# Parting the tail norms' row operations by maxima, and loading the tail's rows and first tile behind the rotation's table

## What is computed

```python
h = _layernorm(x, axis=-1) * (1 + ca) + sa
x = x + ga * _L0_attn_ref(h, W_qkv, b_qkv, W_proj, b_proj)   # causal, 16 heads of 32, rotary q and k
h = _layernorm(x, axis=-1) * (1 + cb) + sb
x = x + gb * _L0_ffn_ref(h, ...)
```

## Time and profile before

| | |
|---|---|
| median of 3 runs | 3283.07 us (3282.28 to 3283.45) |
| profiled execution: its own time | 3289.78 us |
| its span, first to last instruction | 3288.0 us |
| mean granted TensorE clock | 0.962 |
| TensorE busy | 3013.8 us, 92% |
| VectorE busy | 2501.4 us, 76% |
| ScalarE busy | 1849.9 us, 56% |
| GpSimd busy | 1588.9 us, 48% |

### The profile page before, as it was taken

One profiled execution on the slowest core, in us unless ns is written; L12 is line 12 of the kernel. 1 busy time (PEld: TensorE's weight loads), 2 busy tenths in 40 slices (PEclk: granted clock), 3 DMA queues, 4 the chain that ended last, 5 costly groups with the idle time before them and its releaser, 6 DMA issues.

```text
span 3288.0 us, 59164 instructions
## 1 busy us (share of the span) xinstructions
PE 3013.8 (92%) x21664; PEld 1155.9 (35%) x21664; DVE 2501.4 (76%) x4214; ACT 1849.9 (56%) x3651; POOL 1588.9 (48%) x1586
## 2 busy tenths in 40 slices
PE   3799999999989999999998999999998999999896
PEld 1324343434343433434333242433324343242222
DVE  4697777777768788777877878777886878878477
ACT  3416565786655554785455555587545555455541
POOL 2303434482616465382644726365471645627355
PEclk8759999999999999999999999999999999999997
DMA  5403030413041220413113041311314122031122
GB/s 210 107 6 70 11 75 14 101 39 76 14 104 40 61 66 24 98 43 86 39 47 100 27 95 33 80 54 42 83 36 114 39 56 59 30 75 46 55 74 65
DMA packets 180875, 205.27 MB, mean 62 GB/s; under 512 B 21460, under 2 KB 137428, under 8 KB 179428
## 3 DMA queue, kind: packets, MB, share of 16 engines
q1 hardware_dynamic: 180584, 201.50, 23.4%
HBM read 114.09 MB, written 36.50 MB: 46 GB/s over the span
## 4 chain that ended last, share of the span: by engine, by line
PE 46%; issue 19%; DVE 16%; POOL 6%; POOLq 5%; DVEq 3%; ACT 3%; DMA 1%; SPq 1%; ACTq 1%
PE ring L1147 10%; PE ps_out L1197 9%; DVE mpart L902 9%; PE ps_scores L1183 7%; PE ps_scores L1121 5%; PE ps_den L1214 4%; PE ps_den L1220 3%; PE ring L1169 3%; POOL psum L529 3%; PE ps_scores L1133 2%; POOL psum L528 2%; DVE wk L948 1%; DVE dsum L918 1%; DVE wk L946 1%; POOLq L502 1%
## 5 line engine op out<-in xcount | busy, mean ns | idle before, releaser
L730 ACT ACTIVATE prob<-ps_scores 128x512 f32<-128x512 f32 (+3 forms) x2560 | 1257.8, 537 | 981.9 <-PE ps_scores L1186 477.2
L902 DVE TENSOR_REDUCE mpart<-ring 128x1 f32<-128x512 f32 (+3 forms) x2560 | 1403.1, 599 | 344.4 <-PE ring L1147 179.5
L1147 PE MATMUL ring<-qk 96*128 96x512 f16 (+3 forms) x2560 | 876.7, 365 | 73.6 <-DVE mpart L902 56.3
L1183 PE MATMUL ps_scores<-qk 98*128 98x512 f16 (+3 forms) x2560 | 867.2, 352 | 55.7 <-ACT prob L730 28.4
L528 POOL TENSOR_TENSOR psum<-prob 128x512 f32<-128x512 f32 x360 | 481.7, 1338 | 391.9 <-ACT prob L730 299.9
L1197 PE MATMUL ps_out<-prob,v 128*32 128x512 f32 (+3 forms) x5120 | 607.6, 547 | 0.0
L1147 PEld LDWEIGHTS ring<-qk 96*128 96x128 f16 x2560 | 236.1, 98 | 887.3 <-DVE mpart L902 625.2
L529 POOL TENSOR_TENSOR psum<-prob 128x512 f32<-128x512 f32 x360 | 483.4, 1343 | 0.0
L1183 PEld LDWEIGHTS ps_scores<-qk 98*128 98x128 f16 x2560 | 247.1, 99 | 370.1 <-ACT prob L730 215.7
L1121 PE MATMUL ps_scores<-hT,wg 128*128 128x512 f16 x1536 | 345.6, 382 | 3.5 <-POOL hT L519 3.5
L547 POOL TENSOR_TENSOR xs<-xs,bc 128x512 f32<-128x512 f32 x60 | 77.4, 1289 | 383.4 <-DMA xs<-in_L_attn_x_dram 382.1
(11 more groups left out here) (126 smaller groups left out, 2719.7 us busy)
## 6 DMA issues: line engine op xcount, KB each, us to landing
qk<-half SPq DMA_DIRECT2D x384, 128.0 KB, 3.6
turn<-in_rope_dram SPq DMA_DIRECT2D x64, 512.0 KB, 4.7
xs<-in_L_attn_x_dram SPq DMA_DIRECT2D x124, 256.0 KB, 2.8
attn_out_T<-ot SPq DMA_DIRECT2D x63, 256.0 KB, 2.2
otin<-attn_out_T SPq DMA_DIRECT2D x30, 512.0 KB, 4.8
out_dram<-x SPq DMA_DIRECT2D x60, 256.0 KB, 2.1
wg<-w_qkv_halves SPq DMA_DIRECT2D x16, 768.0 KB, 5.6
qk<-in_L_wmod_dram SPq DMA_DIRECT2D x1, 6144.0 KB, 26.8
```

Of the source, the lines that this page charges most:

```text
L730: act.activation(prob[:, s % 3, p, h % 2, 0:w], ps_scores[(HG * s + h) % NBK][:, 0:w], ACT.Exp, scale=SCALE).then_inc(exp_done, 1)
L902: dve.tensor_reduce(mpart[:, h, qt, kc:kc + 1], ring[use % NBK][:, 0:w], AX.X, ALU.max).then_inc(ring_free, 1)
L1147: mm = pe.matmul(ring[use % NBK][:, 0:w], qk[0:R, G % 2, 0, h, qt * P:(qt + 1) * P], qk[0:R, G % 2, 1, h, kc * QC:kc * QC + w], start=True ...
L1183: mm = pe.matmul(ps_scores[k % NBK][:, 0:w], qk[0:RM, par, 1, h, kt * P:(kt + 1) * P], qk[0:RM, par, 0, h, cq * QC + q0:(cq + 1) * QC], st ...
```

## The change

It has two parts. On SyncE, the rows of the modulation are loaded by a function of their own, in the qkv jobs of chunk 0, behind the two DMAs of the maxima rows and before chunk 0's copies; the first tile's loads (otin and x) move behind the table of chunk 3 and the q copies of chunk 2. For batch 3's own tiles the row load stays where it was. On VectorE, parts 2 and 4 of a tail tile issue their first operation only; the second one follows in the same step behind the third and fourth maximum, with the drain ahead of it. The reciprocals of parts 0 and 2 now follow the third maximum, those of parts 1 and 3 and the head's statistics the fourth.

```diff
-            def qkv(G, before, tail_load):
+            def qkv(G, before, row_load, tail_load):
                 for c in range(NC_):
                     if c > 0:
                         stack_halves(G, c - 1, 1)
-                    if c == 2:
-                        tail_load()
                     if G < NG * B - 1 or c < NC_ - 1:
                         load_turn(NC_ * G + c + 1)
                     if c == 0 and before is not None:
                         maxima_rows(before, before % 2)
+                    if c == 0:
+                        row_load()
                     stack_halves(G, c, 0)
+                    if c == 2:
+                        tail_load()
                 stack_halves(G, NC_ - 1, 1)
...
+            def rows_load(b):
+                sp.wait_ge(tail_done, wait_value(NT * b))
+                sp.wait_ge(mod_st, 32)
+                sp.dma_start(bc[:], mod_d[b, 2:8, :].rearrange("(a m) n -> a m n", a=1).to_broadcast(
+                    [P, 6, C])).then_inc(bc_ld, 16)
+
             def tail_loads(b, t, xs_use, count):
                 Z = NT * b + t
-                if t == 0:
-                    sp.wait_ge(tail_done, wait_value(Z))
-                    sp.wait_ge(mod_st, 32)
-                    sp.dma_start(bc[:], mod_d[b, 2:8, :].rearrange("(a m) n -> a m n", a=1).to_broadcast(
-                        [P, 6, C])).then_inc(bc_ld, 16)
...
+                    def row_load():
+                        if 0 in tail.values():
+                            rows_load(b - 1)
...
-                        qkv(NG * b + g + 1, NG * b + g, lambda: tail_load(FIRST_TAIL))
+                        qkv(NG * b + g + 1, NG * b + g, row_load, lambda: tail_load(FIRST_TAIL))
...
+                        if s + 2 in own and own[s + 2] == 0:
+                            rows_load(b)
...
                     dve.wait_ge(tail_rstd1, Z + 1)
                     dve.scalar_tensor_tensor(wk[:, i, :], x1[:, i, :], mv[:, i, 0:1], bc[:, 2, :], ALU.subtract, ALU.mult)
+                elif stage == 3:
                     dve.drain()
-                    dve.scalar_tensor_tensor(wk[:, i, :], wk[:, i, :], rstd[:, i, :], bc[:, 3, :], ALU.mult, ALU.add)
-                    dve.drain()
-                elif stage == 3:
                     dve.bn_stats(stats[:, i, :], wk[:, i, :])
                     dve.drain()
                     dve.bn_aggr(mv2[:, i, :], stats[:, i, :]).then_inc(tail_stats2, 1)
                 else:
-                    tail_third(b, t)
+                    dve.wait_ge(tail_rstd2, Z + 1)
+                    dve.scalar_tensor_tensor(wk[:, i, :], wk[:, i, :], mv2[:, i, 0:1], bc[:, 4, :], ALU.subtract, ALU.mult)
+
+            def tail_second_row(b, t, stage):
+                i = t % 2
+                dve.drain()
+                if stage == 2:
+                    dve.scalar_tensor_tensor(wk[:, i, :], wk[:, i, :], rstd[:, i, :], bc[:, 3, :], ALU.mult, ALU.add)
+                else:
+                    dve.wait_ge(tail_x1_shift, NT * b + t + 1)
+                    dve.scalar_tensor_tensor(x1[:, i, :], wk[:, i, :], rstd2[:, i, :], xs[:, i, :], ALU.mult,
+                                             ALU.add).then_inc(tail_done, 1)
...
-                        out_parts(G, g, s, (0, 2), first, bool(own))
                         for u, h in units[2:3]:
                             unit_max(h, u, n)
                             n += 1
+                        out_parts(G, g, s, (0, 2), first, bool(own))
+                        for u, h in units[3:4]:
+                            unit_max(h, u, n)
+                            n += 1
+                        for stage in (2, 4):
+                            if s - 2 * stage in tail:
+                                tail_second_row(b - 1, tail[s - 2 * stage], stage)
                         if s + 2 in head:
...
-                        for u, h in units[3:]:
+                        for u, h in units[4:]:
```

More of the change, by code:

```diff
@@ L467, in _ @@
             load_turn(0)
-            qkv(0, None, lambda: None)
+            qkv(0, None, lambda: None, lambda: None)
             load_group(1)
```

## The result

The changed kernel takes 3263.36 us (median of 5 runs, 3261.23 to 3268.94) beside 3282.28 us for the kernel before on the same chip: a ratio of 0.995, 95% interval 0.9939 to 0.996. It is faster, by 19 us where 40 were forecast.

A forecast was written before the change was run, and what follows sets the result against it. TensorE was taken as the bound, busy 3013.8 of 3288.0 us. Loads net 24.1 plus row pairs 20.3 gave 44.4 off 3289.8, so 3245.4; less 2.4, 3243. Own range 3226 to 3258; 8 in 10, 3224 to 3268.

The forecast's parts named there:

- the removed cost of the table: Steps 0 to 2 of nine stages: excess over a clean stage goes once the rotation table loads earlier, 38.2 us.
- step 30 of the six-tile stages: Projection's bank comes free earlier: 1.7 us in each of three stages, plus 2.5 for one fallen clock.
- step 24: Five-tile stages: third maximum ahead of the second row, with GpSimd quiet, gains 0.66 us a stage.
- Signs of "wrong": ScalarE's copy wait up over 25 us, TensorE idle in first stages' qkv jobs, stalls one matmul later, long step 0 ScalarE wait.
- the two single rivals: First, row pairs give nothing: 3263, chance 0.15. Second, copies stand behind the whole row load: 3264, chance 0.13.
- the tile loads: Standing between chunk 2's two sets of copies, they hold back the second set: 5.1 us lost over six stages.
- the third rival: Chunk 2's second copies land late behind tile loads, holding step 1's exponentials: 9.7 us each of six stages, 3297, chance 0.05.
- the row load: Ahead of chunk 0's copies it delays them 3.3 us; 3.0 us lost per first stage, 9.0 in all.
- the pairs: Third maximum before the second row: steps 16, 20, 24, 34 gain 2.26 us per five-tile stage; pairs total 20.3.
- in all other such steps there are two or fewer and nothing is parted: Outside the listed steps with a row pair, at most two maxima occur, so the new order changes nothing.
- Step 18: Six-tile stages: VectorE waits for the unfilled third maximum, holding up the second row; 0.3 us lost each, 0.9 in all.
- the profile's own: Of the 6.7 us between profiled execution and median, 2.4 us taken as profile excess and subtracted.

The follow-up runs named there:

- experiment 5: Changed kernel with the row load and the first tile's loads both at chunk 0, ahead of the maxima rows: 3240.75 us, ratio 0.9885.
- experiment 9: Changed kernel with all loads at chunk 0, head statistics ahead of the fourth maximum, GpSimd's shift add behind the pair sums: 3220.75 us, ratio 0.9815.
- experiment 2: Kernel before with only the VectorE part of the change (row pairs), loads as before: 3274.49 us, ratio 0.9976.
- experiment 1: Kernel before with only the SyncE part of the change (loads), VectorE as before: 3280.26 us, ratio 0.9999.
- experiment 3: Changed kernel with the head's statistics ahead of the fourth maximum again: 3260.32 us, ratio 0.9933.
- experiment 6: Changed kernel with the diagonal tile's denominators issued before those of the pair sum: 3261.95 us, ratio 0.9946.
- experiment 8: Changed kernel with GpSimd's shift add, for tiles begun at steps 16 and 30, moved behind the pair sums: 3253.93 us, ratio 0.9912.
- experiment 4: Changed kernel with only the row load moved ahead of the two DMAs of the maxima rows: 3253.18 us, ratio 0.9911.
- experiment 10: Changed kernel with all loads at chunk 0, head statistics first, shift add late and diagonal denominators before the pair sum's: 3217.84 us, ratio 0.9807.

## Why the prediction was right and wrong

Right were the sign, the bound (TensorE's waits), the removed cost of the table (38.2 us forecast; 36.6 shown by experiment 5 and 38.1 by experiment 9), step 30 of the six-tile stages (5.1 + 2.5 forecast; 11.45, 8.96 and 8.97 us became 7.12 to 7.13, 8.0 in sum) and step 24 (0.66 forecast, 0.83). Signs of "wrong" came about too: stalls one matmul later, a long ScalarE wait ahead of step 1 and some idle time at chunk 3, while ScalarE's wait for the copies rose by 13.7 us and not by 25. That the time is that of the two single rivals, 3263 and 3264, is chance: neither happened alone. Of the 20.3 us that the first gives up some 13 were lost (experiment 2 left 7), and of the 21 that the second adds the rows took 6; the tile loads took 5 more than forecast, at 1.1 to 1.4 us a stage that starts with tile 0 or 10 and not the third rival's 9.7.

Of the 44.4 us forecast the profiled pair shows 26.4, and some 5 of these come from falls of the clock in the kernel before's execution, in steps where the change moves nothing: step 6 of batch 2's third stage (6.58 us at 0.74, now 4.25 at 1.00) and steps 1, 5 and 6 of batch 3's last stage (2.6 us). The steps that failed:

- **"I add 0.9 for a short fall of the clock: 3.0 us each, 9.0 in all"** (the row load). The delay of the copies was right (3.0 against 3.3), and so were the stalls in sum: 1.7 us each in steps 0 and 1 and 0.4 in chunk 3, where 1.1 in chunk 3 and 1 at the value copy were taken. The clock term failed: 2.9 instead of 0.9 in this execution, and the rows cost 14.9 (13.8 in the windows, 1.1 in chunk 3). That size is partly chance: with the loads in the same place the first stages' windows took 57.0 us in the changed kernel, but 54.8, 55.7, 51.1 and 54.1 in experiments 1, 3, 6 and 8, and TensorE was busy there for 1.1 to 2.9 us a stage more than the 12.1 of experiment 4. So 0.9 was too low each time, though not by as much.
- **"Together 3 x 1.3 + 3 x 0.4 = 5.1"** (the tile loads). Measured 8.6 by experiment 5 against 4, and 10.1 by experiment 9 against 4, without the fall of the clock in experiment 5. The term "inside the 3.0 above" was not inside: the first stages paid another 1.4 each in step 1, on top of the rows. In the tile-5 stages it was 0.9 rather than 0.4. Only the tile-10 stages came near the forecast (1.1 against 1.3).
- **"so about 0.5 is late next: gain 0.6. Step 34 is the same picture: 0.6."** (the pairs) Five-tile stages were to gain 2.26 us each and gained 0.70 - 0.61 + 0.83 + 0.20 = 1.12. The prediction saw that the pair sum is next, but took each stall alone. Steps 17 and 21 hang on the same 15.4 us of GpSimd: what TensorE wins in the first it waits for in the second. It also priced the late sum as idle time only, and not the group that it parts (1.0 us of busy time in steps 21 and 35). Experiments 6, 8 and 10 show both.
- **"in all other such steps there are two or fewer and nothing is parted"**: true of pairs, but the fourth maximum also moved ahead of the head statistics, in stages that have no pair. 4.8 us lost that no term held; experiment 3 gives them back.
- **Step 18, "-0.9"**: it lost nothing (3.81 and 3.80 us). Step 33, which no term held, lost 0.37 in each six-tile stage, and step 35 there 0.21.

The 2.4 us put down to "the profile's own" cannot be tested: the kernel before's profiled execution was 7.5 above the median of the later runs, the changed kernel's was its median, and falls of the clock differ between executions by as much.

## What to carry to other kernels

A load that is taken from ahead of one transfer on a queue goes ahead of another: look for the stretch in which nobody waits for the queue (here 40 us earlier), not for the next free place. Where a stall on one engine's result is removed, follow the next engine in the chain over all steps that it serves without a pause; if its stretch is no shorter, the gain is only lent. When an instruction is moved past a place in the code, list everything that stood between, also in stages where the aim of the change does not occur.

## What the runs showed of the hardware

- The four-head group of 32-column matmuls takes 1.04 to 1.07 us whole at the full clock. Two of the heads alone take 1.05 us, so served two and two, as the sums arrive, it takes 1.96 us, with no idle time in the profile (experiment 6). A late operand that parts such a group looks like work; only the busy time of the line against the kernel before, 233.7 to 219.3 us, shows it.
- The same stall of 2.9 us left the clock at 1.00 in two of three stages and at 0.74 in the third, and in another run at 0.72 to 0.84 in all three (experiment 1). In batch 1's first stage, with the same loads, the first three steps ran at 0.83 in the changed kernel, at 0.91 in experiment 1, at 1.00 in experiment 6 and at 0.74 in experiment 8. A stage can cost 2.5 us more in one execution than in the next without any change in it, so a gain below that in one stage is not read from one profile.
